# The last q tile of the projection moved into the first attention step of a pre-norm layer

## The reference

```python
x = x + attention(layernorm(x))    # 32 query heads of 32, one head of keys and values for all
x = x + layernorm(x) @ w.T + bias  # w: 1024 x 1024, dequantised from 6-bit codes

def attention(y):
    q = (y @ Wq).reshape(b, s, 32, 32);  kv = y @ Wkv;  k, v = kv[..., :32], kv[..., 32:]
    scores = einsum('bqhd,bkd->bhqk', q, k) * 32 ** -0.5
    scores = where(causal, scores + slope[h] * (pos_k - pos_q), -inf)
    return einsum('bhqk,bkd->bqhd', softmax(scores), v).reshape(b, s, 1024) @ Wo
```

## Time and profile before

| | |
|---|---|
| median of the timed runs | 813.16 us (813.12 to 813.87) |
| the profiled execution | 815.87 us |
| its span, first to last instruction | 814.1 us |
| TensorE busy | 802.0 us, 99% |
| VectorE busy | 594.1 us, 73% |
| ScalarE, GpSimd busy | 370.3 us (45%), 428.5 us (53%) |

### The profile page before, as it was taken

One profiled execution on the slowest core, in us unless ns is written; L12 is line 12 of the kernel. 1 busy time (PEld: TensorE's weight loads), 2 busy tenths in 40 slices (PEclk: granted clock), 3 DMA queues, 4 the chain that ended last, 5 costly groups with the idle time before them and its releaser, 6 DMA issues.

```text
span 814.1 us, 13658 instructions
## 1 busy us (share of the span) xinstructions
PE 802.0 (99%) x4624; PEld 583.3 (72%) x4624; DVE 594.1 (73%) x1594; ACT 370.3 (45%) x728; POOL 428.5 (53%) x311
## 2 busy tenths in 40 slices
PE   7999999999999999999999999999999999999998
PEld 5788888888656555656565655688887788888886
DVE  5885575657878889988888896364737768684878
ACT  2757355321566776667666665221401231041322
POOL 1000000000489988898898988431746387464465
PEclk9999999999999999999999999999999999999999
DMA  9867676566555555565467635452063613510112
GB/s 345 308 212 256 221 243 233 180 191 188 160 136 143 134 147 152 152 156 134 127 171 167 163 101 186 152 168 90 1 234 130 227 44 98 187 39 1 39 66 104
DMA packets 71534, 125.85 MB, mean 155 GB/s; under 512 B 7476, under 2 KB 16980, under 8 KB 71384
## 3 DMA queue, kind: packets, MB, share of 16 engines
q1 hardware_dynamic: 70592, 123.53, 49.5%
q10 hardware_dynamic: 872, 1.45, 0.5%
HBM read 85.61 MB, written 38.94 MB: 153 GB/s over the span
## 4 chain that ended last, share of the span: by engine, by line
PE 88%; DMA 4%; DVE 4%; issue 2%; POOL 1%; ACT 1%; ACTq 0%; SPq 0%; DVEq 0%; POOLq 0%
PE p_s L877 12%; PE p_st L906 10%; PE p_o L917 10%; PE p_o L816 7%; PE p_s L816 6%; PE p_o L930 5%; PE p_s L985 5%; PE p_s L986 5%; PE p_s L987 5%; PE p_o L818 3%; DMA inv_b<-inv_d 3%; PE p_s L818 3%; PE p_st L985 2%; PE p_st L986 2%; PE p_st L987 2%; PE p_s L1009 2%
## 5 line engine op out<-in xcount | busy, mean ns | idle before, releaser
L1496 DVE CUSTOM_DVE_ANT_0 spill<-p_s,mask 128x128 bf16<-128x128 f32 (+3 forms) x512 | 219.5, 483 | 41.6 <-PE p_s L877 41.5
L1198 ACT ACTIVATE pt<-p_st 128x512 f32<-128x512 f32 (+1 forms) x352 | 178.1, 562 | 101.8 <-PE p_st L906 101.6
L645 POOL TENSOR_SCALAR_AFFINE_SELECT pt<-pt 128x512 f32<-128x512 f32 x128 | 88.5, 704 | 234.9 <-ACT pt L1198 234.9
L877 PE MATMUL p_s<-kst,xt 98*128 98x128 f32 (+3 forms) x512 | 151.3, 343 | 0.9 <-DVE mx L1496 0.7
L906 PE MATMUL p_st<-xt,kst 100*128 100x512 f32 (+1 forms) x352 | 129.7, 388 | 0.3 <-ACT pt L1198 0.2
L877 PEld LDWEIGHTS p_s<-kst,xt 98*128 98x128 f32 x512 | 91.7, 189 | 52.7 <-DVE mx L1496 42.3
L652 POOL TENSOR_TENSOR pt<-pt 128x1536 f32<-128x1536 f32 x32 | 112.2, 3507 | 2.7
L917 PE MATMUL p_o<-pt,vst 128*32 128x512 f32 (+3 forms) x1024 | 83.0, 441 | 0.0
L658 POOL TENSOR_TENSOR pt<-pt 128x1024 f32<-128x1024 f32 x32 | 76.7, 2396 | 0.0
L906 PEld LDWEIGHTS p_st<-xt,kst 100*128 100x128 f32 x352 | 64.8, 191 | 13.7 <-issue 5.5
L816 PE MATMUL p_o<-xt,wqh 128*128 128x512 f32 x136 | 53.1, 400 | 0.8 <-DVE xt L1667 0.8
(11 more groups left out here) (212 smaller groups left out, 1621.6 us busy)
## 6 DMA issues: line engine op xcount, KB each, us to landing
xt<-qh_d SPq DMA_DIRECT2D x64, 256.0 KB
qh_d<-qh SPq DMA_DIRECT2D x32, 256.0 KB, 2.1
ql_d<-ql SPq DMA_DIRECT2D x32, 256.0 KB, 2.2
xt<-ql_d SPq DMA_DIRECT2D x32, 256.0 KB
o_d<-o_st SPq DMA_DIRECT2D x32, 256.0 KB, 2.1
ob<-o_d SPq DMA_DIRECT2D x32, 256.0 KB, 4.7
xs<-in_x_t_dram SPq DMA_DIRECT2D x28, 256.0 KB, 5.2
xin<-in_x_dram SPq DMA_DIRECT2D x14, 512.0 KB, 6.0
```

The source lines that it names most:

```text
L645: pool.affine_select(out=own, in_=own, compare_op=ALU.is_ge, fill=0.0, base=0, pattern=[[0, 4], [1, P]], channel_multiplier=-1).then_inc(c ...
L877: pe.matmul(scores_of(n), qst[s % 4][0:R_MAX, j, qb * P:(qb + 1) * P], kst[0:R_MAX, b * S:b * S + keys], start=True, stop=True).then_inc(s ...
L1198: act.activation(pt[s % 2][:, j:j + heads, PT_AT[kb]:PT_AT[kb] + KB_LEN[kb]], p_st[:, place(k) % 3, 0:heads * KB_LEN[kb]].rearrange("p (j ...
L1496: dve.tensor_tensor_reduce(spill[:, SPILL_AT[qb]:SPILL_AT[qb] + keys], scores_of(n), mask[:, S - keys:S], 1.0, LOWEST, ALU.add, ALU.max, m ...
```

## The change

Tiles are numbered from 0 here, as in the code.

- TensorE: tile 7 of the last batch is no longer computed in the projection. Its 24 matmuls are dealt out over step 0 of the attention, one or two ahead of each x and u.
- The first 32 scores, their maxima and the first two turns come a tile earlier (`EARLY` from tile 2 on, not from tile 3).
- VectorE: the last batch's `keys_values` stands behind tile 2, not behind tile 1. Tile 7 is scaled in step 0 behind the 15th maximum, and its low part taken in step 1 behind the eighth.
- ScalarE: the cast of tile 7 comes in step 1, behind its second exponential.
- SyncE: the stores of tile 7 come in step 1, in front of the first load of Wo, and the two stores of maxima each a tile earlier.
- Step 0's exponentials have a buffer of their own, `pt_first`, over x and its raw input, and wait for these alone; step 1's wait for the q products.

```diff
+        with ExitStack() as stage:
+            sb = tensors(stage)
+            sb("up_to_x", [P, 6 * CK + 5, S])
+            pt_first = sb("pt_first", [P, 4, PT_ROW])
...
-        EARLY = {3: (4, 0, 4), 4: (0, 4, 8), 5: (0, 12, 8), 6: (0, 20, 8), 7: (0, 28, 4)}
+        EARLY = {2: (4, 0, 4), 3: (0, 4, 8), 4: (0, 12, 8), 5: (0, 20, 8), 6: (0, 28, 4)}
...
+        def pt_of(s):
+            return pt_first if s == 0 else pt[s % 2]
...
-                for m in range(CK):
-                    if not more and m in (6, 7):
-                        store_max(m - 6)
+                for m in range(CK if more else CK - 1):
+                    if not more and m in (5, 6):
+                        store_max(m - 5)
...
                 if s == 1:
-                    sp.wait_ge(ql_done, CK * B)
+                    store_q(LASTB, CK - 1)
...
-                for m in range(together, CK):
+                for m in range(together, CK if b < LASTB else CK - 1):
...
-                        if b == LASTB and (m, c) == (6, 0):
+                        if b == LASTB and (m, c) == (5, 0):
                             turn_max(0)
-                        if b == LASTB and (m, c) == (7, 5):
+                        if b == LASTB and (m, c) == (6, 5):
                             turn_max(1)
...
+                q_left = [(c, what) for c in range(CK) for what in range(3)] if s == 0 else []
                 for what in ORDER:
+                    for _ in range(2 if len(q_left) > 16 else 1):
+                        if q_left and what in "ux":
+                            queries(LASTB, CK - 1, *q_left.pop(0))
...
                     if s == 0:
+                        act.wait_ge(x_lo, CK * B)
+                        act.wait_ge(sq_done, TILES - TPB)
+                    if s == 1:
                         act.wait_ge(q_done, CK * B)
...
-                    if (s, k) not in ((0, 0), (0, 1)):
-                        exponentials(s, k)
+                    exponentials(s, k)
+                    if (s, k) == (1, 1):
+                        q_high(CK * B - 1)
...
-                    if m == (3 if b == 0 else 1):
+                    if m == (3 if b == 0 else 1 if more else 2):
                         keys_values(b)
...
-                    if s == 0 and i == 11:
+                    if s == 0 and i == 14:
+                        scaled_q(CK * B - 1)
+                    if s == 1 and i == 7:
                         q_low(CK * B - 1)
```

More of the change, by code:

```diff
@@ L402, in load_codes, with store_q @@
                     sp.dma_start(qw[:, :], qw_v[e // 4, max(e % 4 - 1, 0)]).then_inc(qw_in, 16)
+            def store_q(b, m):
+                n = CK * b + m
+                sp.wait_ge(qh_done, n + 1)
+                sp.dma_start(qh_d[b, m], qh[:, m % 2, :].bitcast(F32)).then_inc(q_out[m % 2], 16)
+                sp.wait_ge(ql_done, n + 1)
+                sp.dma_start(ql_d[b, m], ql[:, m % 2, :].bitcast(F32)).then_inc(q_out[m % 2], 16)
             def project(b):
@@ L415, in project @@
                     load_q(0)
-                for m in range(CK):
-                    if not more and m in (6, 7):
-                        store_max(m - 6)
+                for m in range(CK if more else CK - 1):
+                    if not more and m in (5, 6):
+                        store_max(m - 5)
                     if not more and m in (2, 4, 6):
                         load_q(m // 2)
[L421 to L425, removed]
+                    store_q(b, m)
                     if more and m == TURN_M[b] - 1:
@@ L643, in cut @@
                 pool.wait_ge(exp_done, NU * s + UNITS_TO[kb])
-                own = pt[s % 2][:, :, PT_AT[kb]:PT_AT[kb] + P]
+                own = pt_of(s)[:, :, PT_AT[kb]:PT_AT[kb] + P]
                 pool.affine_select(out=own, in_=own, compare_op=ALU.is_ge, fill=0.0, base=0, pattern=[[0, 4], [1, P]],
@@ L648, in add @@
             def add(s, part):
-                p = pt[s % 2]
+                p = pt_of(s)
                 if part == 0:
@@ L917, in values @@
                     last = pe.matmul(p_o[32 * h:32 * h + 32, kb * P:S], vst[:, TPB * b + kb, :],
-                                     pt[s % 2][:, h, PT_AT[kb]:PT_AT[kb] + KB_LEN[kb]], start=(kb == 0), stop=(kb == 3),
+                                     pt_of(s)[:, h, PT_AT[kb]:PT_AT[kb] + KB_LEN[kb]], start=(kb == 0), stop=(kb == 3),
                                      tile_position=(0, 32 * h), skip_group_check=True)
@@ L930, in totals @@
                     last = pe.matmul(p_sum[32 * h:32 * h + 32, to], pick[:, 7 - g:39 - g],
-                                     pt[s % 2][:, h, at:at + to.stop - to.start], start=(g == 0 and part == 0),
+                                     pt_of(s)[:, h, at:at + to.stop - to.start], start=(g == 0 and part == 0),
                                      stop=(g == GROUPS - 1 and part == 1), tile_position=(0, 32 * h), skip_group_check=True)
@@ L1141, in low_weights, with q_high @@
                 act.copy(kv[:, :], p_kv[64:P, :]).then_inc(kv_low, 1)
+            def q_high(n):
+                m = n % CK
+                act.wait_ge(q_freed, n + 1)
+                at_least(act, q_out[m % 2], 32 * (n // 2))
+                act.copy(qh[:, m % 2, :], qt[:, m % 2, :]).then_inc(qh_done, 1)
             def project(b):
@@ L1147, in project @@
                         statistics(4 * b + 4 + t)
-                for m in range(CK):
+                for m in range(CK if more else CK - 1):
                     n = CK * b + m
-                    if not more and m in (6, 7):
-                        max_high(m - 6)
+                    if not more and m in (5, 6):
+                        max_high(m - 5)
                     if not more and m == 5:
                         act.activation(mv[:, 0, 3:4], eps[:, 0:1], ACT.Exp).then_inc(table_in, 1)
-                    if n == CK * B - 1:
-                        exponentials(0, 0)
-                        exponentials(0, 1)
                     if more and m == CK - 1:
@@ L1160, in project @@
                             x_high(b + 1, c)
-                    act.wait_ge(q_freed, n + 1)
-                    at_least(act, q_out[m % 2], 32 * (4 * b + m // 2))
-                    act.copy(qh[:, m % 2, :], qt[:, m % 2, :]).then_inc(qh_done, 1)
+                    q_high(n)
                     if m == (2 if b == 0 else 0):
@@ L1196, in exponentials @@
                     if s == 0:
+                        act.wait_ge(x_lo, CK * B)
+                        act.wait_ge(sq_done, TILES - TPB)
+                    if s == 1:
                         act.wait_ge(q_done, CK * B)
-                act.activation(pt[s % 2][:, j:j + heads, PT_AT[kb]:PT_AT[kb] + KB_LEN[kb]],
+                act.activation(pt_of(s)[:, j:j + heads, PT_AT[kb]:PT_AT[kb] + KB_LEN[kb]],
                                p_st[:, place(k) % 3, 0:heads * KB_LEN[kb]].rearrange("p (j q) -> p j q", j=heads),
@@ L1448, in project @@
                             maximum(EARLY[m][1] + i)
-                            if m == 6 and i == 2:
+                            if m == 5 and i == 2:
                                 max_low(0)
-                    if not more and m == 7:
+                    if not more and m == 6:
                         max_low(1)
@@ L1470, in project @@
                         centre(b + 1, CENTRE[m][0])
-                    if n < CK * B - 1:
-                        q_low(n)
+                    q_low(n)
                     if 0 < b < LASTB and m in (0, 1):
```

## The result

The changed kernel takes 818.43 us (median of 4 runs, 817.70 to 819.53); the kernel before took 813.51 beside it (4 runs, 813.12 to 814.09). The ratio is 1.0063, with an interval of 1.0051 to 1.0075: slower by 4.9 us. The prediction was slower by 3.15, to 816.3, with a range up to 818.2. So the sign was right, and the time lies just above the range.

What follows compares the result with a forecast made beforehand. TensorE, busy for 802.0 of 814.1 us, was taken to bound the kernel. The terms -5.45 + 4.3 + 1.7 + 2.6 gave +3.15 us on the timed median of 813.16, so 816.3 us, range 814.0 to 818.2.

Steps and rivals of the forecast that it cites:

- 1. products leave the projection: Last batch's projection: one q tile's 24 products no longer run there on TensorE, -5.45 us.
- 2. hole at score 8: Fourth tile, last batch's projection: score 8 waits for maxima queued behind keys and values on VectorE, +4.3 us.
- 3. clock in the hole: TensorE's granted clock drops to 0.50 with the wait at score 8: +1.7 us, between 0 and 3.4.
- 4. steps 0 and 1: Attention steps 0 and 1 with the 24 products dealt in, up to the fourth turn of maxima: +2.6 us.
- Rival 1: The clock holds through the wait at score 8: +1.45 us, 814.6 us; chance 0.13.
- Today 19.35 us lie between 210.75 and the fourth turn: Kernel before, as profiled: time from step 0's start at 210.75 to the fourth turn of maxima at 230.10.
- T0 + 21.95: Forecast time of the fourth turn of maxima in the changed kernel, T0 being step 0's new start.
- Edits that I cost at nothing: Last tile's cast, low part and stores in step 1, maxima stores, step 0's own exponentials buffer: taken as 0 us.
- the shift goes on that: The +3.15 us is added to the timed median of 813.16, 2.7 under the profiled 815.87, giving 816.3 us.
- Rival 2: No wait at score 8, VectorE reaching maximum 4 by about 181.35: -2.85 us, 810.3 us; chance 0.13.
- Rival 3: The clock stays low twice as long behind score 8's wait: +4.85 us, 818.0 us; chance 0.12.
- The signs announced: Score 8 waits some 4 us, clock 0.50 behind it, quiet step 0, turns 9.37 apart about 3 us later.

Runs made afterwards that it cites:

- kernel 4: Changed kernel with the last batch's keys and values cut into seven pieces between the maxima and the scalings: 812.15 us, ratio 0.9991.
- kernel 2: Changed kernel with 17 extra products that nobody reads run by TensorE in front of score 8: 816.36 us, ratio 1.0040.
- kernel 3: Changed kernel with the last batch's keys and values back behind tile 1, the rest of the change kept: 816.35 us, ratio 1.0039.
- kernel 8: On top of kernel 4, only the last tile's low part moved two maxima later in step 1: 812.49 us, one run.
- repeated run: The kernel before, unedited, run and profiled once more: 813.08 us, ratio 1.0002; its profiled execution took 813.83 us.
- kernel 6: Changed kernel with all 24 products of the last q tile in one block ahead of step 0's first score: 819.55 us, ratio 1.0075.
- kernels 2 to 5: Kernel 2, kernel 3, kernel 4 and, as the fifth, the changed kernel once more without an edit: 818.61 us, ratio 1.0069.
- kernel 7: On top of kernel 4, last tile's scaling behind step 0's last maximum and low part two maxima later in step 1: 811.24 us, ratio 0.9973.

## Why the prediction came out as it did

| us, tile 2 to the fourth turn | predicted | measured, against the profile read | measured, against a usual execution |
|---|---|---|---|
| 1. products leave the projection | -5.45 | -5.45 | -5.45 |
| 2. hole at score 8 | +4.3 | +4.2 | +4.2 |
| 3. clock in the hole | +1.7 | +1.5 to 1.7 | +1.5 to 1.7 |
| 4. steps 0 and 1 | +2.6 | +2.95 | +4.35 |
| sum | +3.15 | +3.33 | +4.73 |

The sums are differences of rows (61.66 less 58.33 and less 56.93). Term 1 is not measured by itself; with the others it closes each sum within 0.2.

**Terms 1 and 2: right.** Score 8 came 14.46 us behind the start of tile 2, forecast 14.58 (186.35 less 171.77). It was due at 182.33 (the 182.04 of the prediction plus the later start of 0.29), so the hole is 4.2 us. Maximum 4 was forecast at 185.66 and came at 185.82, of which 0.29 is the later start. With the block cut up (kernel 4) the hole is gone, which shows the cause.

**Term 3: right in kind and size.** The windows give 1.7, the difference to kernel 2 gives 1.54. The size was a guess from one earlier drop, so that it fits this well is in part luck. The rule of the Trainium skill ("TensorE: Matmul & The Clock Gate", "Why this matters for your kernels"), that idle gaps between bursts of matmuls bring the clock back to its lower rate, was set against the case that one stop doesn't count. The trace agrees with it, with 0.50 behind the stop. Rival 1, that the clock holds, is refuted for a stop of 4.0 us; at 2.46 us the profiled execution of kernel 3 shows it.

**Term 4: the step that failed**, in "Today 19.35 us lie between 210.75 and the fourth turn". That number is right for the execution that was read and 1.40 us too long for the kernel: the usual one is 17.95. And the other side, "T0 + 21.95", came out at T0 + 22.30 (211.42 to 233.72). The third turn was forecast to 12.6 behind T0 and came at 12.56 (223.98), with 0.53 of the 0.7 us of wait. The 0.35 are all in the next interval, 9.74 for 9.37: the moved low part, among "Edits that I cost at nothing", took 1.59 us instead of 0.69, and kernel 8, which moves it alone, brings the interval back to 9.38. So the term is 22.30 - 17.95 = +4.35, not 2.6.

**The sum: where the first of these errors entered the time.** The execution read took 815.87 us, 2.7 over the median. In its own frame the forecast was good: 819.0, and the profiled execution of the changed kernel took 818.70. What failed is the step "the shift goes on that", the median: I did not ask what the 2.7 were. The two profiles of before, 2.0 us apart, answer most of it. 1.4 us lie from tile 2 to the fourth turn, the clock drop in step 0; 0.3 lie ahead of tile 2; and 0.4 behind the fourth turn, where the wait for GpSimd is 1.1 shorter in the repeated run (1.3 us in the earlier trace rows, now 0.2) and the one for VectorE's `xc` 0.4 longer. The 0.7 by which the repeated profile itself is over 813.16 were not traced. So I took the 1.4 off with the median and took them off again in term 4, as something that the change mends. With that and the low part mended the sum is 813.16 + 4.73 = 817.9, inside the range and 0.5 from the time. Of these 0.5 us, 0.35 are the reference: beside the changed kernel the median of before was 813.51, a fourth run (814.09) having been added, and 813.51 + 4.73 is 818.2. The 0.2 left can't be told from scatter: the ten executions of the changed kernel take 817.70 to 821.51. Three of the ten have a mean clock of 0.995, at 818.40, 819.53 and 821.51 us; none of them was profiled, and the first is the shortest of its six.

**The rivals.** Rival 2 (no hole) did not come; kernel 4 is what it described, with the cause it named, and at 812.15 it is dearer than its 810.3, by 1.4 of the reference and 0.35 of the low part. Rival 3 names nearly the right time, 818.0, but by luck and for a wrong reason: the clock was low for as long as seen before, not twice as long. The signs announced were there: the 4 us wait, the 0.50, a quiet step 0 and turns 9.37 apart from the fourth on (9.38).

## What to carry to other kernels

Before a stretch of a profile is used as "what it costs today", compare the profiled execution with the median, find which stretches hold the excess, and see whether the stretch is one of them; a shift computed inside such a stretch must not be put on the median as it is. When a stage is moved ahead on one engine, look on the engine that frees its buffers for the longest block in front of the first release: the block need not be late for its own user to stop the others, and cut in pieces it stopped no score here. The 4.0 us stop of TensorE cost its length and some 1.5 us of clock behind it, so in this kernel the first place to win was the single long wait, not the sum of the short ones.

## What was not expected of the hardware

**A wait and the clock.** Behind a stop of 4.0 us there is a low stretch in both profiles of the changed kernel and in that of kernel 6, and none of the ten executions of the changed kernel has a full mean clock. Behind a stop of 2.46 us the one profile shows none, while the other five executions have mean clocks of 0.997 and 0.998. Step 0 of before, where TensorE is starved in short waits, has a low stretch in one profile of two, and 2 of 47 further executions have a mean clock as low. So whether a wait costs the clock can differ from one execution to the next of the same kernel: count the mean clocks of all timed runs, and don't take it from one profile.

**VectorE beside GpSimd.** The low part is a subtraction with both inputs in SBUF. In the repeated run of before, VectorE's row, and then GpSimd's, which starts just behind it:

```profile
216.32 0.69 DVE L1440 TENSOR_TENSOR ql<-qt,qh 128x512 fp32r<-128x512 f32 x1
```

```profile
216.36 3.98 POOL L652 TENSOR_TENSOR pt<-pt 128x1536 f32<-128x1536 f32 x1
```

The mean of these adds stands on the page (busy us, mean ns of one, idle before):

```profile
L652 POOL TENSOR_TENSOR pt<-pt 128x1536 f32<-128x1536 f32 x32 | 112.2, 3505 | 2.7
```

VectorE takes its 0.69 us and GpSimd's add 3.98, where the mean of all 32 is 3.51. In the changed kernel it is the other way round:

```profile
227.48 1.59 DVE L1461 TENSOR_TENSOR ql<-qt,qh 128x512 fp32r<-128x512 f32 x1
```

```profile
225.53 2.41 POOL L669 TENSOR_TENSOR pt_first<-pt_first 128x1024 f32<-128x1024 f32 x1
227.88 0.64 POOL L656 TENSOR_SCALAR_AFFINE_SELECT pt<-pt 128x512 f32<-128x512 f32 x1
```

GpSimd's add is under way when the subtraction starts, and a cut of the mask, with one input, follows it. The subtraction ends at 229.07, 0.55 us behind the end of the cut. So it does in kernels 2 to 5, by 0.54 or 0.55 us. In kernel 8, where the subtraction starts only during the cut, the cut runs from 221.92 to 222.56 and the subtraction ends at 223.10; in kernel 7 it runs to 222.73 and the subtraction ends at 223.28: 0.54 and 0.55. So in these kernels the subtraction does next to nothing until GpSimd is through with the cut too. But GpSimd does not always go on to its second instruction first. In kernel 6 the subtraction comes in between:

```profile
229.03 1.52 DVE L1460 TENSOR_TENSOR ql<-qt,qh 128x512 fp32r<-128x512 f32 x1
```

```profile
227.59 2.40 POOL L669 TENSOR_TENSOR pt_first<-pt_first 128x1024 f32<-128x1024 f32 x1
229.94 1.10 POOL L656 TENSOR_SCALAR_AFFINE_SELECT pt<-pt 128x512 f32<-128x512 f32 x1
```

It ends at 230.55, 0.56 behind the add, and now the cut takes 1.10 us instead of 0.64. What decides between the two no run shows. The Trainium skill ("SBUF — State Buffer", "SBUF: two separate sides") says that such an operation and a GpSimd operation that reads SBUF exclude each other, and that the one which starts first keeps the port for all of its instruction. The traces agree, with 0.69 us for the subtraction where it starts first and 1.02 to 1.59 where it starts second. I had costed the moved instruction by its duration where it stood before, where it came first.
